# Another order and spacing of weight transforms in a two-layer kernel, three groups begun on GpSimd

## The chip, the cores and the metric

The kernel runs on 1 core of one Trainium2 chip. The metric is the device time in microseconds of one execution; the figure is the median over several. Engines are called PE (TensorE), DVE (VectorE), ACT (ScalarE), POOL (GpSimd) and SP (SyncE, which here only issues transfers).

## The reference, cut to what matters

2048 tokens of width 512 go through four blocks, each on the layer norm of the running x and added to x:

```
x = x + scan(ln(x))      # state space scan, 16 states per channel
x = x + ffn(ln(x))       # x' = fwht(x * SU)/64 ; silu(x' Wg^T) * (x' Wu^T) ; fwht ; Wd^T
x = x + mixer(ln(x))     # ((x Wx^T) conv^T * D) * silu(x Wz^T), then Wout^T
x = x + moe(ln(x))       # 64 experts, top 8, capacity 128
```

fwht is the Walsh-Hadamard transform over the last dimension. The kernel moves both transforms from the activations onto the weights: W_gate, W_up (u groups) and W_down (d groups) are transformed once, while the scan of the first tokens runs, and stored to HBM. In the same way W_in and conv_w of the mixer are multiplied into one matrix (the folds).

## The kernel before, in words

The tokens are done in 4 chunks of 512. The scan of a chunk takes 16 states, n = 0 to 15, and its work is spread over 4 places per state. A place is a number, pos = 5 + 64c + 4n + m for chunk c, state n and m = 0 to 3; (n,m) is used for a place of chunk 0. Each engine's program runs over the places in the same order, and at each one `side(pos)` issues the work of the other blocks that a table puts there. Engines are held together by semaphores alone.

In state n, DVE does **bx** (L1268, u times the broadcast of B in a PSUM bank), side(n,0), two scans (L1277), side(n,1), two scans, side(n,2), **hc** (L1295, bx times the broadcast of C), side(n,3). hc(n) below is its end. ACT makes the decay factors of the four blocks (L940); the one of block k waits for scan k-2, and blocks 2 and 3 stand between side(n,0) and side(n,1), blocks 0 and 1 of the next state ahead of side(n,3). PE makes the broadcasts of B (L662) and C (L670); the C broadcast of state n waits for hc(n-1). POOL adds hc to y (L1453). In chunk 0 PE and ACT also prepare chunk 1: transposes (ACT L902) in states 5 and 6, the product xdbl (PE L682) in state 7, softplus (ACT L912 to L923) in states 9 and 10.

Side work of chunk 0:

* **Preps.** A prep is one 128x512 tile of a transformed weight, 4 to a group, and there are 8 u groups and 4 d groups. PE does four fp32 matmuls with a plus or minus Hadamard matrix into a bank (L632), at the prep's place. One place later ACT writes the rounded hi part (L871, L874) and DVE the rest, the **lo** part (L1157, L1162). Two places later SP stores both (L382, L385), once the lo is done. The staging of d has two slots, so its hi waits for the store of the prep two before.
* **Butterflies.** A d group is first scaled and summed on POOL, in place: part 0 is one operation of 128x2048 (L1473), parts 1 and 2 are two of 128x1024 each (L1483). The next raw_d is loaded after the group's last prep. The table `butterflies` gives the place of each part.
* **Plains.** 16 tiles of W_in and W_out only split in hi (ACT L878, in fst) and lo (POOL L1489, one place later); SP stores them 3 places after, behind the prep's store of that place. fst has two slots: the hi of plain i waits for the store of plain i-2 (`mixer_hi`).
* **Folds.** 4 in chunk 0, places in `fold_at`: 8 matmuls each of winx and conv (L644), hi on ACT (L878), lo on DVE (L1169). SP loads conv (L410) and winx (L453) two places after the last prep's place, behind the wait for its lo, its store and the wait for its matmuls. At place 61 SP starts to load transformed weights back (ring).

Before: the preps have the places 3 to 50, one each, in the order u d u u u d u u d u u d; the plains have 7, 10, 13 to 52; the folds 58, 61, 64, 67.

Of the kernel before, what the change touches and what calls it, by code (L numbers as in the profile page):

```python
# [13 lines left out]
P = 128  # L14
# [3 lines left out]
KT = D // P  # L18
# [34 lines left out]
def build(nc, a):  # L53
# [5 lines left out]
    ALU, ACT, AX = mybir.AluOpType, mybir.ActivationFunctionType, mybir.AxisListType  # L59
    ds = bass.ds  # L60
    top = ExitStack()
    sem = lambda n: top.enter_context(nc.semaphore(n))

    def wait(eng, s, v):

        if not (isinstance(v, int) and v <= 0):
            eng.wait_ge(s, v)

    def sb(ctx, name, shape, dt=fp32):
        return ctx.enter_context(nc.sbuf_tensor(name, shape, dt))  # L70
# [30 lines left out]
    with top:  # L101
# [20 lines left out]
        with A:  # L122
# [32 lines left out]
            with ExitStack() as prep_only:  # L155
                staged_u = sb(prep_only, "staged_u", [P, 2, 4, 512], f32r)
                staged_d = sb(prep_only, "staged_d", [P, 2, 2, 512], f32r)
                raw_u = sb(prep_only, "raw_u", [P, 2, 4, 512])
                raw_d = sb(prep_only, "raw_d", [P, 2, M0 * P])
                wsdp = sb(prep_only, "wsdp", [P, D])  # L160
                had = sb(prep_only, "had", [P, 2, P])
            rawd, sums = raw_d[:, 0, :], raw_d[:, 1, :]
            ring = sb(A, "ring", [P, RING, 2 * D], f32r)
            expert_buffers((4,))
# [43 lines left out]
            PB, PC, dA, PF = bank[0], bank[1], bank[2:4], bank[4:8]  # L208
# [2 lines left out]
            S_x = [sem(f"x_in{c}") for c in range(NCH)]; S_id = sem("identity_in"); S_w = sem("weights_in")  # L211
            S_raw = [sem("raw_in0"), sem("raw_in1")]; S_rawd = sem("raw_down_in")
            S_wsc = sem("raw_scaled"); S_pmm = sem("prep_mm"); S_ph = sem("prep_hi"); S_pl = sem("prep_lo")
            S_bf = sem("butterfly"); S_sel = sem("selectors")
            S_su = [sem(f"up_stored{i}") for i in range(4)]; S_sd = [sem(f"down_stored{i}") for i in range(2)]
            S_wx = sem("winx_in"); S_cv = sem("conv_in"); S_pr = [sem(f"plain_in{i}") for i in range(4)]
            S_fm = sem("fold_mm"); S_mh = sem("mixer_hi"); S_fl = sem("fold_lo"); S_wl = sem("plain_lo")
# [24 lines left out]
            state_at = lambda c, n, m: HEAD + SPAN * c + 4 * n + m  # L242
# [27 lines left out]
            for place in range(TAIL, TAIL + RING):  # L270
                del quanta_at[place]

            kinds = [w for w in "uduuuduuduud"]
            group_of = [kinds[:i].count(kinds[i]) for i in range(len(kinds))]
            prep_places = list(range(3, 3 + 4 * len(kinds)))
            prep_at = {place: (i // 4, i % 4) for i, place in enumerate(prep_places)}
            fold_at = {state_at(0, 13, 1) + 3 * m: (0, m) for m in range(KT)} | {state_at(1, 1, 0) + 2 * m: (1, m) for m in range(KT)}
            FOLDS, PLAINS = 2 * KT, 2 * M1
            plain_at = {state_at(0, 0, 2) + 3 * i: i for i in range(PLAINS)}

            borrowed_b, borrowed_c = {}, {}
            for c in range(NCH):
# [56 lines left out]
            with nc.Block() as block:  # L339
# [17 lines left out]
                def _(sp):  # L357
# [17 lines left out]
                    def store_prep(i, m):  # L375

                        g = group_of[i]
                        sp.wait_ge(S_pl, 4 * i + m + 1)
                        if kinds[i] == "u":
                            for part in range(2):  # L380
                                dst = gate_up[g // 4, 4 * (g % 4):4 * (g % 4) + 4, :, m, part, :].rearrange("t p c -> p t c")
                                sp.dma_start(dst, staged_u[:, part, m, :].rearrange("p (t c) -> p t c", t=4).bitcast(fp32)).then_inc(S_su[m], 16)  # L382
                        else:
                            for part in range(2):
                                sp.dma_start(down_ffn[m, part, g],  # L385
                                             staged_d[:, m % 2, part, :].rearrange("p (x c) -> p x c", x=4).bitcast(fp32)).then_inc(S_sd[m % 2], 16)
# [55 lines left out]
                    def prep(pos):  # L442
                        if pos - 2 in prep_at:
                            i, m = prep_at[pos - 2]
                            store_prep(i, m)
                            g = group_of[i] + (2 if kinds[i] == "u" else 1)
                            if m == 3 and g < kinds.count(kinds[i]):
                                sp.wait_ge(S_pmm, 4 * i + 4)
                                load_raw(kinds[i], g)
                            if (i, m) == (len(kinds) - 1, 3):  # L450
                                sp.wait_ge(S_pmm, 4 * len(kinds))
                                load_conv(0)
                                sp.dma_start(winx[:, :, :], a["winx"].rearrange("(k p) h -> p k h", p=P)).then_inc(S_wx, 16)  # L453
                        if pos - 2 in fold_at:
                            half, m = fold_at[pos - 2]
                            sp.wait_ge(S_fl, KT * half + m + 1)
                            store_mixer(PLAINS + KT * half + m)
                            if half == 0 and m == KT - 1:
                                load_conv(1)
# [36 lines left out]
                    for pos in range(LAST):  # L496
# [11 lines left out]
                        if state_at(1, 8, 0) <= pos < state_at(3, 0, 0) and (pos - state_at(1, 8, 0)) % 6 == 0:  # L508
                            n = (pos - state_at(1, 8, 0)) // 6
# [46 lines left out]
                def _(pe):  # L556
# [65 lines left out]
                    def prep(i, m):  # L622
                        g = group_of[i]
                        if kinds[i] == "u":
                            pe.wait_ge(S_raw[g % 2], 16 * (g // 2 + 1))
                        else:
                            pe.wait_ge(S_bf, 4 * g + 4)
                        wait(pe, S_pl, 4 * (i - 1) + m + 1)
                        for k in range(4):
                            x = raw_u[:, g % 2, k, :] if kinds[i] == "u" else \  # L630
                                rawd.rearrange("p (x m h) -> p x m h", x=4, m=4)[:, :, k, :]
                            last = nc.tensor.matmul(PF[m][:, :], had[:, 0 if H4[m][k] > 0 else 1, :], x,  # L632
                                                    start=(k == 0), stop=(k == 3))
                        last.then_inc(S_pmm, 1)
# [811 lines left out]
                def _(pool):  # L1446
# [38 lines left out]
                    def plain_lo(i):  # L1485
                        pool.wait_ge(S_mh, i + 1)
                        s = i % 2
                        wait(pool, S_ms[s], 32 * (i // 2))
                        nc.gpsimd.tensor_tensor(fst[:, s, 1, :], praw[:, i % 4, :], fst[:, s, 0, :].bitcast(fp32),  # L1489
                                                ALU.subtract).then_inc(S_wl, 1)  # L1490

                    def correction(c, k):

                        pool.wait_ge(S_rs, KT * c + k + 1)
                        pool.wait_ge(S_rel, KT * c + k + 1)
                        nc.gpsimd.tensor_tensor(spc[:, k % 2, :], dl[c % 2][:, k, :], spc[:, k % 2, :], ALU.subtract).then_inc(S_co, 1)
                        pool.wait_ge(S_co, KT * c + k + 1)
                        nc.gpsimd.tensor_tensor(spr[:, k, :], spr[:, k, :], spc[:, k % 2, :], ALU.add).then_inc(S_sp, 1)
# [6 lines left out]
                    def states(c):  # L1505
                        for n in range(NS):
                            for m in range(4):
                                side(state_at(c, n, m))
                                if state_at(c, n, m) - 1 in plain_at:
                                    plain_lo(plain_at[state_at(c, n, m) - 1])  # L1510
                                if c >= 1 and (n, m) == (1, 2):
                                    norm_rstd(pool, n2, c - 1)
                                if c >= 1 and (n, m) == (14, 0):
                                    norm_rstd(pool, n3, c - 1)
                                if c + 1 < NCH:
                                    if (n, m) == (4, 1):
                                        norm_rstd(pool, n1, c + 1)
                                    if n in (9, 10) and m == 3:
                                        correction(c + 1, 2 * n - 18)
                                        correction(c + 1, 2 * n - 17)  # L1520
                                    if (n, m) == (13, 1):
                                        softplus_sum(c + 1)
                                if c == 0 and (n, m) in butterflies:
                                    butterfly(*butterflies[n, m])
                            add(c, n)

                    butterflies = {(2, 1): (1, 0), (3, 1): (1, 1), (4, 1): (1, 2), (6, 1): (2, 0), (6, 3): (2, 1), (7, 1): (2, 2),
                                   (9, 0): (3, 0), (9, 1): (3, 1), (10, 0): (3, 2)}

                    def rows_out(i, k):  # L1530
                        if (i, k) == (0, 0):
# [93 lines left out]
```

## Time and profile before

| | |
|---|---|
| median of 3 runs (lowest, highest) | 1737.85 us (1732.64, 1740.98) |
| the profiled execution, its own time | 1744.28 us |
| its span, first to last instruction | 1742.4 us |
| mean granted TensorE clock | 0.940 of full |
| busy: PE, DVE, POOL, ACT | 86%, 61%, 46%, 33% of the span |

The busy shares are means over stages that differ. Chunk 0, where the changed work lies, is the first sixth of the span; the last third belongs to the experts. A time in the trace counts from the span's start.

### The profile page before, as it was taken

How to read it: one execution, taken by the hardware profiler on the slowest of the kernel's cores; microseconds unless marked ns; L12 is line 12 of the kernel's file. 1: busy time of each engine (PE TensorE's matmuls, PEld its weight loads, DVE VectorE, ACT ScalarE, POOL GpSimd, SP SyncE). 2: the span in 40 equal slices, each digit the busy share in tenths (PEclk: the TensorE clock that was granted, in tenths of full speed). 3: DMA queues.
4: the chain of work that ended last, by engine and by line, in shares of the span. 5: the costliest groups of instructions: out<-in, count | busy, mean ns of one | idle time of the engine just before them, and what ended most of it. 6: DMA issues, size and time to landing. Idle time of an engine off the chain costs nothing. (4 is left out here: it accounts for less than half of the span.)

```text
span 1742.4 us, 19092 instructions
## 1 busy us (share of the span) xinstructions
PE 1506.9 (86%) x5792; PEld 1038.0 (60%) x5792; DVE 1062.9 (61%) x1591; ACT 583.2 (33%) x1034; POOL 794.6 (46%) x491
## 2 busy tenths in 40 slices
PE   6989966899948899988999899999991799998992
PEld 2444323577736677766887787778771455554551
DVE  4887688887898987889988746452553122222220
ACT  4434633344534335343433322121210232222220
POOL 3467853354744445634644326662376232222222
PEclk8999988999969999999999999999995899999996
DMA  6899663356644677766655468997760799999987
GB/s 202 251 280 277 194 217 132 101 156 196 199 140 149 201 221 222 216 192 225 187 183 169 145 201 305 351 317 227 227 191 25 227 329 317 311 306 301 307 211 126
DMA packets 193541, 380.41 MB, mean 218 GB/s; under 512 B 20994, under 2 KB 95106, under 8 KB 192944
## 3 DMA queue, kind: packets, MB, share of 16 engines
q1 hardware_dynamic: 165360, 322.89, 59.8%
q0 software_dynamic: 20032, 39.92, 9.7%
q10 hardware_dynamic: 8064, 16.55, 2.8%
q8 instruction: 42, 0.69, 0.2%
q14 instruction: 43, 0.35, 0.1%
HBM read 301.65 MB, written 124.35 MB: 244 GB/s over the span
## 5 line engine op out<-in xcount | busy, mean ns | idle before, releaser
L1453 POOL TENSOR_TENSOR y<-y,hc 128x2048 f32<-128x2048 f32 x64 | 293.3, 4582 | 250.3 <-DVE hc L1295 250.3
L590 PE MATMUL bank<-tokT,ring 128*128 128x512 f32 x768 | 307.9, 401 | 12.9 <-DVE xall L1150 6.9
L1277 DVE TENSOR_TENSOR_SCAN bx<-bank,state,bx 128x512 f32<-128x512 f32 x256 | 312.6, 1267 | 0.8
L592 PE MATMUL bank<-tokT,ring 128*128 128x512 f32 x768 | 302.3, 394 | 0.0
L591 PE MATMUL bank<-tokT,ring 128*128 128x512 f32 x768 | 302.2, 393 | 0.0
L940 ACT ACTIVATE bank<-dl,an 128x512 f32<-128x512 f32 x256 | 171.0, 684 | 330.4 <-DVE bx L1277 330.3
L1459 POOL TENSOR_TENSOR act<-th,act 128x512 fp32r<-128x512 f32 x96 | 126.4, 1316 | 269.6 <-ACT act L864 269.1
L819 PE MATMUL bank<-wgu,xeT 128*128 128x384 f32 x512 | 181.0, 498 | 0.0
L590 PEld LDWEIGHTS bank<-tokT,ring 128*128 128x128 f32 x768 | 146.2, 190 | 49.2 <-issue 17.6
L602 PE MATMUL bank<-ring,act 128*128 128x512 f32 x360 | 147.6, 410 | 22.6 <-DVE th L1139 17.3
L592 PEld LDWEIGHTS bank<-tokT,ring 128*128 128x128 f32 x768 | 146.0, 190 | 32.1
L591 PEld LDWEIGHTS bank<-tokT,ring 128*128 128x128 f32 x768 | 146.1, 190 | 29.4
L1295 DVE TENSOR_TENSOR hc<-bx,bank 128x2048 f32<-128x2048 f32 x64 | 146.0, 2282 | 22.7 <-PE bank L670 22.0
L1268 DVE TENSOR_TENSOR bx<-u,bank 128x2048 f32<-128x2048 f32 x64 | 146.0, 2281 | 9.5 <-PE bank L662 6.3
L1535 POOL DMA_INDIRECT slots<-row,idx x128 | 126.4, 987 | 38.4 <-issue 35.9
L604 PE MATMUL bank<-ring,act 128*128 128x512 f32 x360 | 143.4, 398 | 0.0
L603 PE MATMUL bank<-ring,act 128*128 128x512 f32 x360 | 143.3, 398 | 0.0
L1569 POOL DMA_INDIRECT out<-ye,tok x32 | 49.4, 1542 | 187.6 <-ACT ye L1087 110.5
L1132 DVE SCALAR_TENSOR_TENSOR th<-th,bank 128x512 f32<-128x512 f32 x96 | 65.7, 684 | 99.9 <-ACT th L859 88.9
L819 PEld LDWEIGHTS bank<-wgu,xeT 128*128 128x128 f32 x512 | 94.3, 194 | 53.5 <-issue 4.4
L836 PE MATMUL bank<-wde,hT 96*128 96x512 f32 x256 | 120.6, 593 | 0.5 <-DVE hT L1435 0.5
L632 PE MATMUL bank<-raw_u,had 128*128 128x512 f32 x256 | 115.5, 601 | 0.5 <-DMA raw_u<-wgT_in 0.5
(147 smaller groups left out, 2007.9 us busy)
## 6 DMA issues: line engine op xcount, KB each, us to landing
ring<-w_all SPq DMA_DIRECT2D x288, 512.0 KB
wgu<-wgu_in SPq DMA_DIRECT2D x64, 768.0 KB
wde<-wd_in SPq DMA_DIRECT2D x64, 384.0 KB
slots<-empty_in SPq DMA_DIRECT2D x16, 1154.0 KB, 8.7
w_all<-staged_u SPq DMA_DIRECT2D x64, 256.0 KB, 3.2
xe<-slots ACTq DMA_DIRECT2D x56, 288.5 KB
w_all<-fst SPq DMA_DIRECT2D x48, 256.0 KB, 3.7
w_all<-staged_d SPq DMA_DIRECT2D x32, 256.0 KB, 3.7
```

What stands on the lines that cost most here:

```text
L590: nc.tensor.matmul(b[:, :], w[:, k, 0, :], x[:, 0, k, :], start=(k == 0), stop=False)
L591: nc.tensor.matmul(b[:, :], w[:, k, 0, :], x[:, 1, k, :], start=False, stop=False)
L592: last = nc.tensor.matmul(b[:, :], w[:, k, 1, :], x[:, 0, k, :], start=False, stop=(k == KT - 1))
L602: nc.tensor.matmul(PF[t][:, :], act8[:, 0, j, tok], w[:, 0, :], start=(j == 0), stop=False)
L603: nc.tensor.matmul(PF[t][:, :], act8[:, 0, j, tok], w[:, 1, :], start=False, stop=False)
L604: last = nc.tensor.matmul(PF[t][:, :], act8[:, 1, j, tok], w[:, 0, :], start=False, stop=(j == pairs - 1))
L819: last = nc.tensor.matmul(CG[i % 2][:, 0:2 * FE], xeT[:, i % 2, k, :], wgu[i][:, k, :], start=(k == 0), stop=(k == KT - 1))
L940: nc.scalar.activation(dA[k % 2][:, :], dl[c % 2][:, k, :], ACT.Exp, scale=an[:, k, n:n + 1]).then_inc(S_dA, 1)
L1268: nc.vector.tensor_tensor(bx[:, :, :], u[:, :, :], PB[:, :].unsqueeze(1).to_broadcast([P, KT, CH]), ALU.mult).then_inc(S_bm, 1)
L1277: nc.vector.tensor_tensor_scan(bx[:, k, :], dA[k % 2][:, :], bx[:, k, :], state[:, k, n:n + 1], ALU.mult, ALU.add).then_inc(S_sc, 1)
L1295: nc.vector.tensor_tensor(hc[:, :, :], bx[:, :, :], PC[:, :].unsqueeze(1).to_broadcast([P, KT, CH]), ALU.mult).then_inc(S_cm, 1)
L1453: nc.gpsimd.tensor_tensor(y[c % 2][:, :, :], y[c % 2][:, :, :], hc[:, :, :], ALU.add).then_inc(S_ya, 1)
```

## The change

The order of the groups and the places of preps, plains, butterflies and folds are changed. The u groups with index 2, 5 and 8 are done in two stages: POOL forms the sums and differences of the raw halves (two operations of 128x1024 each, in a new tile `paired`), and a prep of these groups is then two matmuls of those. Its raw_u tile is loaded anew after the two sums and not after the matmuls. The Hadamard signs come out the same: rows 0 and 1 need the sums, rows 2 and 3 the differences.

```diff
+                paired = sb(prep_only, "paired", [P, 2, 2, 512])
-            kinds = [w for w in "uduuuduuduud"]
+            kinds = [w for w in "uduuduuduuud"]
-            prep_places = list(range(3, 3 + 4 * len(kinds)))
+            prep_places = [3 + 50 * i // 47 for i in range(4 * len(kinds))]
-            fold_at = {state_at(0, 13, 1) + 3 * m: (0, m) for m in range(KT)} | {state_at(1, 1, 0) + 2 * m: (1, m) for m in range(KT)}
+            PAIRED = [2, 5, 8]
+            paired_before = {i: PAIRED.index(i) for i in PAIRED}
+            pairs_at = {prep_places[4 * i] - 4 + 2 * part: (i, part) for i in PAIRED for part in range(2)}
+            fold_at = {state_at(0, 13, 2) + 5 * m // 2: (0, m) for m in range(KT)} | {state_at(1, 1, 0) + 2 * m: (1, m) for m in range(KT)}
-            plain_at = {state_at(0, 0, 2) + 3 * i: i for i in range(PLAINS)}
+            plain_at = {place: i for i, place in enumerate((7, 9, 11, 13, 20, 22, 24, 26, 32, 34, 36, 50, 52, 54, 56, 58))}
...
-                            if m == 3 and g < kinds.count(kinds[i]):
-                                sp.wait_ge(S_pmm, 4 * i + 4)
+                            if m == (0 if i in paired_before else 3) and g < kinds.count(kinds[i]):
+                                if i in paired_before:
+                                    sp.wait_ge(S_pd, 2 * paired_before[i] + 2)
+                                else:
+                                    sp.wait_ge(S_pmm, 4 * i + 4)
                                 load_raw(kinds[i], g)
...
+                        if i in paired_before:
+                            for k in range(2):
+                                last = nc.tensor.matmul(PF[m][:, :], had[:, k * (m % 2), :], paired[:, m // 2, k, :],
+                                                        start=(k == 0), stop=(k == 1))
+                            last.then_inc(S_pmm, 1)
+                            return
...
+                    def pair_sums(i, part):
+                        g = group_of[i]
+                        pool.wait_ge(S_raw[g % 2], 16 * (g // 2 + 1))
+                        if i != PAIRED[0]:
+                            pool.wait_ge(S_pmm, 4 * PAIRED[paired_before[i] - 1] + 2 * part + 2)
+                        nc.gpsimd.tensor_tensor(paired[:, part, :, :], raw_u[:, g % 2, 0:2, :], raw_u[:, g % 2, 2:4, :],
+                                                ALU.subtract if part else ALU.add).then_inc(S_pd, 1)
...
-                    butterflies = {(2, 1): (1, 0), (3, 1): (1, 1), (4, 1): (1, 2), (6, 1): (2, 0), (6, 3): (2, 1), (7, 1): (2, 2),
-                                   (9, 0): (3, 0), (9, 1): (3, 1), (10, 0): (3, 2)}
+                    butterflies = {(2, 1): (1, 0), (2, 3): (1, 1), (3, 1): (1, 2), (5, 2): (2, 0), (6, 0): (2, 1), (6, 2): (2, 2),
+                                   (9, 0): (3, 0), (9, 3): (3, 1), (10, 2): (3, 2)}
```

Written out, the preps of after have the places 3 to 18, 20 to 35, 37 to 51 and 53 (19, 36 and 52 are empty). The d groups stand at 7 to 10, 20 to 23, 32 to 35 and 49, 50, 51, 53; the paired u groups at 11 to 14, 24 to 27 and 37 to 40, and their pair sums at 7 and 9, 20 and 22, 33 and 35. The folds stand at 59, 61, 64 and 66.

## Rows read from the trace of the kernel before

**Rows 1.** Instructions in time on DVE, chunk 0: start, duration, operation, idle before.

```profile
44.95 2.29 DVE L1268 TENSOR_TENSOR bx<-u,bank 128x2048 f32<-128x2048 f32 x1
...
97.91 2.28 DVE L1295 TENSOR_TENSOR hc<-bx,bank 128x2048 f32<-128x2048 f32 x1
...
131.51 2.29 DVE L1295 TENSOR_TENSOR hc<-bx,bank 128x2048 f32<-128x2048 f32 x1
...
164.21 2.29 DVE L1295 TENSOR_TENSOR hc<-bx,bank 128x2048 f32<-128x2048 f32 x1 [1.14 <-PE bank L670]
...
208.65 0.75 DVE L1157 SCALAR_TENSOR_TENSOR staged_u<-bank,vec,staged_u 128x512 fp32r<-128x512 f32 x1 [5.29 <-ACT staged_u L871]
...
216.03 2.29 DVE L1295 TENSOR_TENSOR hc<-bx,bank 128x2048 f32<-128x2048 f32 x1 [3.33 <-PE bank L670]
...
282.83 2.28 DVE L1268 TENSOR_TENSOR bx<-u,bank 128x2048 f32<-128x2048 f32 x1
```

**Rows 2.** Stretch table: length, busy PE, PEld, DVE, ACT, POOL, clock, DMA share, GB/s.

```profile
44.90:226.20 181.30, 173.56 (x418) 77.89 (x416) 140.94 (x126) 87.40 (x152) 121.10 (x52) 0.98 0.85 247
```

**Rows 3.** Instructions in time on DVE, states 2 and 12.

```profile
74.25 2.28 DVE L1268 TENSOR_TENSOR bx<-u,bank 128x2048 f32<-128x2048 f32 x1
...
80.98 0.75 DVE L1157 SCALAR_TENSOR_TENSOR staged_u<-bank,vec,staged_u 128x512 fp32r<-128x512 f32 x1 [1.43 <-ACT staged_u L871]
...
87.51 2.28 DVE L1268 TENSOR_TENSOR bx<-u,bank 128x2048 f32<-128x2048 f32 x1
...
231.46 2.29 DVE L1268 TENSOR_TENSOR bx<-u,bank 128x2048 f32<-128x2048 f32 x1 [0.20 <-DVE hc L1295]
...
241.17 2.29 DVE L1268 TENSOR_TENSOR bx<-u,bank 128x2048 f32<-128x2048 f32 x1 [0.20 <-DVE hc L1295]
```

**Rows 4.** Instructions in time on PE, states 2 to 4.

```profile
80.53 0.79 PE L662 MATMUL bank<-xdr,sel 128*128 128x512 f32 x1
...
95.47 0.80 PE L662 MATMUL bank<-xdr,sel 128*128 128x512 f32 x1
...
111.00 5.40 PE L632 MATMUL bank<-raw_d,had 128*128 128x512 f32 x8 [4.21 <-POOL raw_d L1483]
```

**Rows 5.** Instructions in time, winx load (SP), fold 0 (PE) and its lo (DVE).

```profile
230.64 0.85 SPq L453 DMA_DIRECT2D winx<-winx_in  x1
...
245.31 8.52 PE L644 MATMUL bank<-conv,winx 128*128 128x512 f32 x16 [3.49 <-DMA winx<-winx_in]
...
254.50 0.69 DVE L1169 TENSOR_TENSOR fst<-bank,fst 128x512 fp32r<-128x512 f32 x1 [6.20 <-ACT fst L878]
```

**Rows 6.** The page's costliest groups: busy, mean ns of a record, idle before.

```profile
L632 PE MATMUL bank<-raw_u,had 128*128 128x512 f32 x256 | 115.5, 601 | 0.5 <-DMA raw_u<-wgT_in 0.5
```

**Rows 7.** Instructions in time, POOL and DVE in the head.

```profile
23.25 9.55 POOL L1483 TENSOR_TENSOR raw_d<-raw_d 128x1024 f32<-128x1024 f32 x4
...
30.63 2.72 DVE L1197 TENSOR_TENSOR spc<-dl,spc 128x512 f32<-128x512 f32 x1
...
34.45 0.69 DVE L1197 TENSOR_TENSOR spc<-dl,spc 128x512 f32<-128x512 f32 x1
```

**Rows 8.** Instructions in time, POOL and PE in states 6 and 7.

```profile
149.97 4.53 POOL L1453 TENSOR_TENSOR y<-y,hc 128x2048 f32<-128x2048 f32 x1
153.48 3.60 PE L682 MATMUL bank<-y,wxp 128*128 128x512 f32 x8
154.46 4.66 POOL L1483 TENSOR_TENSOR raw_d<-raw_d 128x1024 f32<-128x1024 f32 x2
```

**Rows 9.** DMA issues of the whole run: size, median us to landing.

```profile
winx<-winx_in SPq DMA_DIRECT2D x1, 2048.0 KB, 14.6
```

**Rows 10.** DMA queue and issues of 59 to 104 us.

```profile
q1 hardware_dynamic: 20813, 12.86, 101.4%
...
w_all<-fst SPq DMA_DIRECT2D x8, 256.0 KB, 4.8
```

**Rows 11.** Instructions in time on ACT, state 1.

```profile
67.21 0.60 ACT L874 ACTIVATE staged_d<-bank 128x512 fp32r<-128x512 f32 x1 [1.57 <-DMA w_all<-staged_d]
```

More of the change, by code:

```diff
@@ L213, in build @@
             S_wsc = sem("raw_scaled"); S_pmm = sem("prep_mm"); S_ph = sem("prep_hi"); S_pl = sem("prep_lo")
-            S_bf = sem("butterfly"); S_sel = sem("selectors")
+            S_bf = sem("butterfly"); S_pd = sem("pairs_summed"); S_sel = sem("selectors")
             S_su = [sem(f"up_stored{i}") for i in range(4)]; S_sd = [sem(f"down_stored{i}") for i in range(2)]
@@ L624, in prep @@
                         if kinds[i] == "u":
-                            pe.wait_ge(S_raw[g % 2], 16 * (g // 2 + 1))
+                            if i in paired_before:
+                                pe.wait_ge(S_pd, 2 * paired_before[i] + m // 2 + 1)
+                            else:
+                                pe.wait_ge(S_raw[g % 2], 16 * (g // 2 + 1))
                         else:
@@ L628, in prep @@
                         wait(pe, S_pl, 4 * (i - 1) + m + 1)
+                        if i in paired_before:
+                            for k in range(2):
[3 more added lines that the diff above has]
+                            return
                         for k in range(4):
@@ L1510, in states @@
                                     plain_lo(plain_at[state_at(c, n, m) - 1])
+                                if state_at(c, n, m) in pairs_at:
+                                    pair_sums(*pairs_at[state_at(c, n, m)])
                                 if c >= 1 and (n, m) == (1, 2):
```

## The prediction

> **What bounds the kernel now.** I read the busy table by stretches first, then VectorE (DVE) in order of time, then the engines it waits for. Every step the change touches lies in the head or in chunk 0, between the first bx at 44.95 us and chunk 1's first at 282.83 [rows 1]; up to place 53 TensorE (PE) looks like the bound: 173.6 us busy of 181.3, DVE 140.9 [rows 2]. The reader should distrust that share. In state 2, with four preps and no late input, DVE goes from bx to bx in 87.51 - 74.25 = 13.26 us, of which 1.43 is a wait for ScalarE (ACT) [rows 3]: the hi half of the prep at (n,0) stands on ACT behind the decay of block 3, and that behind DVE's second scan, while DVE does this prep's lo before its third scan. That wait is there however fast PE is. PE's own period with four preps is 95.47 - 80.53 = 14.94 [rows 4]. So PE exceeds the DVE-ACT loop by only 1.7 us a state, and may run up to some 6.6 us ahead (its next prep is needed only after a lo, bx, a lo, two scans and a decay: 0.7 + 2.2 + 0.7 + 2.4 + 0.7 by the same rows). A state without preps takes 241.17 - 231.46 = 9.7 [rows 3], so four lo cost 13.26 - 1.43 - 9.7 = 2.1, 0.53 each. Shorter preps alone therefore give back little; what counts is where DVE waits for PE, GpSimd (POOL) or a DMA, and where the chunk ends: PE waits for winx, the fold comes late, DVE stands 6.20 us [rows 5].
>
> **The change, part by part.** Times are of the profiled execution (span 1742.4, own time 1744.28, which is 6.4 above the median 1737.85); I carry the difference to the median.
>
> *Removed:* 3 groups x 4 preps x 2 matmuls = 24 fp32 matmuls. 128 such instructions make 256 records and 115.5 us busy, 0.90 each [rows 6]; between the broadcasts at 80.53 and 95.47 an unhindered prep of four takes some 3.43, 0.86 each, so 20.6 us of PE. Six POOL pair sums of 128x1024 come in, 2.37 each by the butterfly's row (9.55 for four of that size) [rows 7], 14.2 us. ACT and DVE do exactly as much as before.
>
> *Head.* The first pair sum (place 7) waits for nothing but the second raw_u load, one of the first transfers of all. POOL does it right behind the first butterfly, at 32.8 us. There DVE has its first softplus, and the rows show what meets: the subtraction that overlaps the last butterfly takes 2.72 us against 0.69 for the same one later, and ends 0.5 us after POOL [rows 7]. DVE is the chain there. A 2.37 us pair sum started in one of its gaps costs between 0 and 2.4; I take 2: **+2.0**. The trace shows two operands in SBUF on both sides. The Trainium skill, page SBUF — State Buffer, section "SBUF: two separate sides", states the rule: a DVE operation with two SBUF inputs and a GpSimd operation that reads SBUF hold the shared port pair exclusively, and the later one blocks for the whole instruction; by it this sum costs up to 2.4, and the other five nothing, since scans, bx, hc and lo read one operand from PSUM. The trace agrees (2.72 against 0.69); the sum above goes by the rows alone.
>
> *hc(3) to hc(5)* (100.19 to 133.80, each the start plus 2.28 or 2.29) [rows 1]: PE's 4.21 us wait for butterfly g1 [rows 4] goes, since the butterfly now runs before norm_rstd; place 19 is empty. DVE then needs, in state 4, 9.7 + 1.6 (three lo) + 3.9 for chunk 1's statistics + 1.3 ACT wait + 0.6 plain = 17.0 or so, and in state 5 9.7 + 2.1 + 3.1 (ACT wait with two evacuations and a plain ahead of the hi) = 14.9: 31.9 for 33.6: **-1.7**.
>
> *hc(5) to hc(7)* (133.80 to 166.50 = 32.7) [rows 1]: group 7 (d) begins at place 32 and needs butterfly g2, whose parts 1 and 2 both stand behind add(5). The chain is add 4.54, four butterfly halves 2 x 4.68 [rows 8], two preps 7.0, xdbl 3.4 [rows 8], two preps 6.5, broadcasts 0.9, hc 2.3: 34.1: **+1.4**.
>
> *hc(7) to hc(11)* (166.50 to 231.26, where hc(11) ends 0.2 before bx(12)) [rows 1, 3]: state 8 has one lo fewer, -0.3. In states 9 and 10 the long waits (5.29 in state 10) are ACT's softplus, six activations ahead of the hi, and stay; hc(10)'s wait of 3.33 for the C broadcast, on PE itself behind butterfly g3, goes [rows 1], with 0.6 for a plain no longer there and 1.4 of small PE waits: -5.3. State 11 gets a plain before its hi: +0.6. Together **-5.0**.
>
> *hc(11) to chunk 1.* Before, the winx load was issued at 230.64, 0.6 before hc(11), and PE started fold 0 at 245.31, when it had landed [rows 5]; 14.6 is its time to landing, conv ahead of it [rows 9]. Both loads stand in SP's program behind the store of the **last prep**, now place 53 = (12,0), whose lo DVE does at (12,1): after hc(11) a lo, bx, two scans, a decay, a plain and a hi (with its DMA wait), a lo: 8.4; store and two issues 1.5: winx at +9.9, landed +24.5. Fold 0 takes 8.0 to the next broadcast, folds 1 and 2 with their broadcasts 7.3 each, fold 3 7.0, hi and lo 1.4, delta_x 2.3, hc 2.3, bx: +60.9. Before: 282.83 - 231.26 = 51.6. **+9.3**. DVE arrives at its fold 0 lo at about +21.8 and stands some 12 us, where it stood 6.20 [rows 5]. The later fold places (59, 61, 64, 66) don't help: the data is late, not the place.
>
> Sum so far: 2.0 - 1.7 + 1.4 - 5.0 + 9.3 = **+6**.
>
> *Plains.* Before they were 3 places apart, now 2 in bunches. A plain's hi on ACT waits for the store of the plain two before, which SP issues 3 places after that plain, behind a prep's store. At spacing 2 that leaves one place. Queued behind ACT's wait are the prep's hi and the decays, and DVE waits for those. No such wait is in the trace (spacing 3 hides it): its lower bound is 0. In 59 to 104 us the queue is full (101.4%) and an fst store lands in 4.8 [rows 10]; a staged_d store issued behind a raw_u load held ACT until 67.21 [rows 11], some 7.6 after its issue. lo, two issues and landing make 5.7 to 9; ACT is there 3.9 to 5 after the lo. Plain 2: 1; plain 3, behind both the raw_d and the raw_u load that now fall in places 12 and 13: 4 to 6; plains 6 and 10: 2 each; upper end 12. Nearest to the rows taken in the full queue I take **+9**. Plains 13 to 15 fall under the winx wait and cost nothing; were it gone, plain 14's wait for a store queued behind 4.2 MB would show.
>
> After chunk 0 the program is the same and takes its start from it, so the sum passes on: **+15**, 1752.9.
>
> **Rivals.**
> *A. The plain waits are hidden* (DVE slack or quick stores), the head partly: +4 to +6, 1743. For it: ACT is idle a third of each state. Against: the full queue.
> *B. PE is the bound throughout* and ACT's wait is only its echo: the 20.6 us come off wholly before hc(11), the winx term stays: 20.6 - 9.3 = -11.3, 1726.6. It decides if states with paired preps fall to about 10 us. For it: the 173.6 of 181.3. Against: the 13.26 with PE on time.
> *C. The queue decides:* what is full now is asked for in bunches; every store that ACT waits for takes 7.6 or more, the plain term goes from 9 to 12 and the butterflies' d loads and the winx landing take some 2 more each: +22, 1760.
> *D. The change doesn't do what it says:* Hadamard rows 0,1 and 2,3 share sums and differences, so two matmuls suffice, and each is awaited by its own pair count; no chance worth a number.
>
> **Numbers.** About 0.5% (8.7 us) is what a measurement of this kernel can tell from no change. Forecast (+9 to +19) 0.50, A 0.25, B 0.12, C 0.13. Slower: forecast and C, 0.62 with the edge taken off; same: A and that edge, 0.26; faster: B, 0.12. The range goes from below A's end, -4, to C's near part, +27: 1734 to 1765.
>
> **What would show it.** In the profile after: bx(1,0) near 297 us instead of 282.8; winx issued near 9 to 10 us after hc(11) and fold 0's lo preceded by 10 to 14 us idle on DVE; no L632 wait for raw_d at states 4 and 10; one softplus operation of some 2.4 us more in the head; new ACT waits of fst on a DMA, the longest in state 2; states with paired preps still near 13 us. If those states take 10 to 11, the argument is wrong; if no ACT fst line names a DMA, the plain term is; if winx is issued before hc(11) + 5, the tail is.

## The result and the profile after

The changed kernel took 1764.63 us (median of 4, 1748.59 to 1768.74) where the kernel before took 1735.24; the ratio is 1.0147, 95% interval 1.0092 to 1.0202. It is slower. The medians lie 29 us apart, the ratio makes it some 25, and 15 were forecast; the median lies 0.4 us inside the upper end of the range (1765), so that the range held by luck. Timed again, the changed kernel took 1758.81 us, ratio 1.014 (below). Its profiled execution has a span of 1766.9 us for the 1742.4 before. Chunk 0 is 18.0 us of these 24.5.

DVE in order of time, after (start, duration, operation, idle before and its releaser), to be laid beside [rows 1, 3, 5]; L1284 is bx, L1293 the scan, L1311 hc, L1173 the u lo, L1185 the fold lo:

```profile
46.75 2.29 DVE L1284 TENSOR_TENSOR bx<-u,bank 128x2048 f32<-128x2048 f32 x1
...
84.36 0.75 DVE L1173 SCALAR_TENSOR_TENSOR staged_u<-bank,vec,staged_u 128x512 fp32r<-128x512 f32 x1 [6.94 <-ACT staged_u L887]
...
105.83 2.28 DVE L1311 TENSOR_TENSOR hc<-bx,bank 128x2048 f32<-128x2048 f32 x1
...
138.22 0.75 DVE L1173 SCALAR_TENSOR_TENSOR staged_u<-bank,vec,staged_u 128x512 fp32r<-128x512 f32 x1 [5.16 <-ACT staged_u L887]
...
141.90 2.28 DVE L1311 TENSOR_TENSOR hc<-bx,bank 128x2048 f32<-128x2048 f32 x1
...
177.60 2.29 DVE L1311 TENSOR_TENSOR hc<-bx,bank 128x2048 f32<-128x2048 f32 x1 [1.35 <-PE bank L686]
...
237.66 2.28 DVE L1311 TENSOR_TENSOR hc<-bx,bank 128x2048 f32<-128x2048 f32 x1
...
266.32 2.46 DVE L1293 TENSOR_TENSOR_SCAN bx<-bank,state,bx 128x512 f32<-128x512 f32 x2 [8.83 <-ACT bank L956]
...
274.03 0.69 DVE L1185 TENSOR_TENSOR fst<-bank,fst 128x512 fp32r<-128x512 f32 x1 [2.88 <-ACT fst L894]
...
300.84 2.29 DVE L1284 TENSOR_TENSOR bx<-u,bank 128x2048 f32<-128x2048 f32 x1 [0.20 <-DVE hc L1311]
```

From the ends of hc, the stretches of the forecast come out like this (us; the forecast's plain term is put where the plains are; "again" is the second profile of the changed kernel, from the experiment further down):

| stretch | before | after | change | forecast | again |
|---|---|---|---|---|---|
| start to first bx | 44.95 | 46.75 | +1.8 | +2.0 | 46.90 |
| to hc(3) | 55.2 | 61.4 | +6.1 | +5 to 7 (5 in the sum) | 61.7 |
| hc(3) to hc(5) | 33.6 | 36.1 | +2.5 | +0.3 | 36.1 |
| hc(5) to hc(7) | 32.7 | 35.7 | +3.0 | +1.4 | 34.0 |
| hc(7) to hc(11) | 64.8 | 60.1 | -4.7 | -3.0 | 60.1 |
| hc(11) to chunk 1's first bx | 51.6 | 60.9 | +9.3 | +9.3 | 60.3 |
| sum | | | +18.0 | +15 | |

The 24 matmuls are gone all the same: in chunk 0 PE is busy 10 us less than before, in 16 us more. Stretch table, kernel before and then after (length, busy PE, PEld, DVE, ACT, POOL, clock, DMA share, GB/s):

```profile
44.95:282.83 237.88, 207.23 (x490) 92.34 (x488) 188.04 (x158) 110.14 (x188) 146.35 (x59) 0.94 0.79 235
```

```profile
46.75:300.84 254.09, 197.07 (x437) 86.15 (x435) 188.79 (x158) 109.37 (x188) 156.71 (x64) 0.88 0.75 224
```

The granted clock of the stretch fell from 0.94 to 0.88 of full, so that part of the time saved is given back at 1.2 GHz; PE is idle for 57 us of the stretch, before for 31.

The head, DVE and POOL in time, beside [rows 7]:

```profile
30.42 2.72 DVE L1213 TENSOR_TENSOR spc<-dl,spc 128x512 f32<-128x512 f32 x1
33.17 2.72 DVE L1215 TENSOR_TENSOR spr<-spr,spc 128x512 f32<-128x512 f32 x1
```

```profile
32.55 2.80 POOL L1514 TENSOR_TENSOR paired<-raw_u 128x1024 f32<-128x1024 f32 x1
```

A second softplus operation now takes 2.72 us for 0.69, and it ends 0.5 us after the pair sum.

ACT in time. Before, no ACT instruction waited for an fst store; after, six plains do:

```profile
70.53 0.63 ACT L894 ACTIVATE fst<-praw 128x512 fp32r<-128x512 f32 x1 [2.32 <-DMA w_all<-fst]
...
83.12 0.63 ACT L894 ACTIVATE fst<-praw 128x512 fp32r<-128x512 f32 x1 [9.58 <-DMA w_all<-fst]
...
265.07 0.63 ACT L894 ACTIVATE fst<-praw 128x512 fp32r<-128x512 f32 x1 [12.09 <-DMA w_all<-fst]
```

The first two are plains 2 and 3, the last plain 14. The chunk's waits by pair of engines (in total, times, longest) add up to:

```profile
ACT fst L894 <- DMA w_all<-fst: 29.2, 6, 12.1
```

Two of the others are plain 6 (1.78 us, at 126.00) and plain 7, which the forecast did not have:

```profile
136.98 0.63 ACT L894 ACTIVATE fst<-praw 128x512 fp32r<-128x512 f32 x1 [2.13 <-DMA w_all<-fst]
```

The tail, SP and PE in time, beside [rows 5]:

```profile
249.36 0.83 SPq L460 DMA_DIRECT2D winx<-winx_in  x1
```

```profile
252.56 0.80 PE L686 MATMUL bank<-xdr,sel 128*128 128x512 f32 x1 [9.28 <-DVE hc L1311]
263.78 9.59 PE L660 MATMUL bank<-conv,winx 128*128 128x512 f32 x16 [10.42 <-DMA winx<-winx_in]
```

hc(11) ends at 239.94, so winx is issued 9.4 after it (forecast 9.9) and fold 0 starts 23.8 after it (forecast 24.5).

### The profile page after: what moved, and what is told of

Read it like the earlier page. It is cut to its first block and busy times, and to the rows that moved or that the text cites. A ratio compares the mean times of both kernels' runs of the same rounds, so it can differ in the third digit from the quotient of the medians.

```text
span 1766.9 us, 19006 instructions
## 1 busy us (share of the span) xinstructions
PE 1501.3 (85%) x5744; PEld 1035.7 (59%) x5744; DVE 1065.6 (60%) x1591; ACT 582.9 (33%) x1034; POOL 808.7 (46%) x497
## 5 line engine op out<-in xcount | busy, mean ns | idle before, releaser
L1293 DVE TENSOR_TENSOR_SCAN bx<-bank,state,bx 128x512 f32<-128x512 f32 x256 | 312.7, 1266 | 9.7 <-ACT bank L956 8.8
L1311 DVE TENSOR_TENSOR hc<-bx,bank 128x2048 f32<-128x2048 f32 x64 | 145.9, 2280 | 20.7 <-PE bank L686 20.0
L1284 DVE TENSOR_TENSOR bx<-u,bank 128x2048 f32<-128x2048 f32 x64 | 145.9, 2279 | 13.1 <-PE bank L678 10.2
L1438 DVE TENSOR_SCALAR wsc<-xe 128x1 f32 (+1 forms) x64 | 9.7, 152 | 162.2 <-DMA out<-ye,tok 94.7
```

Source lines behind the costliest of these rows:

```text
L1284: nc.vector.tensor_tensor(bx[:, :, :], u[:, :, :], PB[:, :].unsqueeze(1).to_broadcast([P, KT, CH]), ALU.mult).then_inc(S_bm, 1)
L1293: nc.vector.tensor_tensor_scan(bx[:, k, :], dA[k % 2][:, :], bx[:, k, :], state[:, k, n:n + 1], ALU.mult, ALU.add).then_inc(S_sc, 1)
```

## The experiments

Chunk 0 repeats far better than the whole: two profiles of the kernel before have chunk 1's first bx at 282.83 and 282.82, two of the changed one at 300.84 and 299.12. So this instant is read in each profile, and the whole time is weighed only where rounds were run. Gains on the changed kernel are given against its first profile, 300.84; against its second, 299.12, each is 1.7 us less. The difference lies mostly in the stretch from hc(5) to hc(7) (35.7 and 34.0).

**Plains back at their old places.**

```diff
-            plain_at = {place: i for i, place in enumerate((7, 9, 11, 13, 20, ...))}
+            plain_at = {state_at(0, 0, 2) + 3 * i: i for i in range(PLAINS)}
```

> The changed kernel with the plains back at their old places, 3 apart (7, 10 to 52), nothing else. Chunk 1's first bx stands at 300.8 us in the changed kernel and at 282.8 before. Theory (ACT waits for the fst store of the plain two before, and DVE for ACT): the 6.9 us idle of DVE in state 2 goes, 1.6 between states 4 and 5, and some 2 in state 5; the ACT wait of 12.1 us for plain 14 in states 12 and 13 goes too, but there the winx load takes over. First bx of chunk 1 near 291, the kernel 9 to 11 us faster than the changed one. Rival (the transfer queue is full because of the raw loads, whatever the plains do): at most 3 us faster, 298 or later.

Measured: first bx of chunk 1 at 293.75, 7.1 earlier; one run 1750.65. DVE in time, the lo in state 2 and the first fold lo:

```profile
77.96 0.75 DVE L1173 SCALAR_TENSOR_TENSOR staged_u<-bank,vec,staged_u 128x512 fp32r<-128x512 f32 x1
...
266.92 0.69 DVE L1185 TENSOR_TENSOR fst<-bank,fst 128x512 fp32r<-128x512 f32 x1 [11.24 <-ACT fst L894]
```

The 6.94 us in state 2 are gone, and no ACT plain waits for a transfer any more. The gain is below the expected 9 to 11. Up to hc(5) it is 8.5 us, where 10.5 were expected, and from hc(5) to hc(7) it takes 37.7 us for 35.7: PE comes earlier to the next d group, waits 4.37 us for its butterfly (3.13), and its 16 records take 9.56 us. What plain 14's wait had cost DVE (8.83 us) turns wholly into waiting for the fold (11.24 for 2.88): the two lay under one another, as forecast.

**Loads early.** conv and winx no longer stand behind the last prep. winx's memory overlaps the preparation buffers, so these were put in another order, with a gap of 2816 words before winx, and what is left to overlap is raw_u's second slot and `paired`, done with after group 10:

```diff
-                            if (i, m) == (len(kinds) - 1, 3):
-                                sp.wait_ge(S_pmm, 4 * len(kinds))
-                                load_conv(0)
-                                sp.dma_start(winx[:, :, :], ...)
+                        if pos == 43:
+                            load_conv(0)
+                        if pos == 51:
+                            sp.wait_ge(S_pmm, 44)
+                            sp.dma_start(winx[:, :, :], ...)
```

> The changed kernel with conv loaded at place 43 and winx at place 51 (behind the matmuls of group 10 alone), made possible by another order of the preparation buffers and a gap ahead of winx; nothing else is moved. Theory (the fold is late because its loads stand behind the last prep's store): PE no longer waits 10.4 us for winx, DVE's scans of state 13 no longer 8.8 us for ACT, since plain 12's store isn't queued behind 4 MB; from hc(11) to chunk 1's first bx 60.9 us become 48 to 52, first bx near 290. Rival (the folds' own PE time and places set it): 57 or more, first bx at 297 or later.

Measured: first bx at 294.27, 6.6 earlier; from hc(11) 54.3 us for the 60.9. The rival (57 or more) falls, but the gain is smaller than expected, and DVE shows why:

```profile
251.48 0.69 DVE L1180 TENSOR_TENSOR staged_d<-bank,staged_d 128x512 fp32r<-128x512 f32 x1 [5.54 <-ACT staged_d L892]
```

The winx load now runs in front of plain 11's store, ACT waits 3.61 for that, and the last prep's lo comes 5.5 late. The wait moved; part of it was paid twice.

**First pair sum one place later.**

```diff
+            pairs_at = {prep_places[4 * i] - 4 + 2 * part + (i == 2 and part == 0): (i, part) ...}
```

> The changed kernel with the first pair sum one place later (8), so that POOL does it behind plain 0's lo and not during DVE's first softplus. Theory (two operations with both operands in SBUF don't overlap): the second softplus operation takes 0.69 us and not 2.72, chunk 0's first bx is back from 46.75 to 44.95, all behind it 1.8 us earlier. Rival (the delay is from ACT or PE): no change at chunk 0's first bx.

Measured: chunk 0's first bx at 44.83 (1.9 earlier), and the second softplus operation 0.69. That part is shown. But chunk 1's first bx is at 295.36, 5.5 earlier and not 1.8: plain 3's wait fell from 9.58 to 7.98, and another 1.7 came off between hc(5) and hc(7). The latter is scatter: that stretch is 34.0 us here and in the changed kernel's second profile too. Why a shift of 1.9 us shortens plain 3's wait wasn't followed up.

**No pairs.**

```diff
-            PAIRED = [2, 5, 8]
+            PAIRED = []
```

> The changed kernel without pair sums: all preps are four matmuls again, order and places stay. Theory (PE isn't the bound in these states; the loop of DVE and ACT is): head 1.8 us earlier, the preps' states at most some 4 us longer in all, first bx of chunk 1 between 299 and 303. Rival (PE is the bound, and the pairs have saved 20.6 us that something else ate): first bx at 315 or later.

Measured, DVE in time:

```profile
44.75 2.29 DVE L1284 TENSOR_TENSOR bx<-u,bank 128x2048 f32<-128x2048 f32 x1
...
299.32 2.29 DVE L1284 TENSOR_TENSOR bx<-u,bank 128x2048 f32<-128x2048 f32 x1 [0.20 <-DVE hc L1311]
```

With 24 matmuls more the chunk takes 254.57 us for 254.09 (252.22 in the changed kernel's second profile). The pairs save 0.5 to 2.4 us behind the first bx, where 20.6 us of PE were taken out, and cost 2.0 in the head. State 8, whose four preps are all paired in the changed kernel, takes 12.7 us from bx to bx with pairs (180.41 to 193.14) and without (177.35 to 190.07). PE as the bound (315 or later) falls for this schedule.

**The new plain places alone, on the kernel before.**

```diff
-            plain_at = {state_at(0, 0, 2) + 3 * i: i for i in range(PLAINS)}
+            plain_at = {place: i for i, place in enumerate((7, 9, 11, 13, 20, ...))}
```

> The kernel before with the changed kernel's plain places (7, 9, 11, 13, 20 to 26, 32, 34, 36, 50 to 58) and nothing else of the change. Theory: the ACT waits for fst stores appear here too, so the cost belongs to the bunching and not to pairs or group order; chunk 1's first bx goes from 282.8 to between 288 and 294, with one ACT wait of 6 to 10 us near state 2. Rival (the raw_d and raw_u loads that the changed kernel puts into neighbouring places make the wait): less than 3 us, 286 or earlier.

Measured: first bx at 294.36, 11.5 later than before, at the upper end; one run 1758.14 beside 1737.16. ACT in time:

```profile
80.00 0.63 ACT L878 ACTIVATE fst<-praw 128x512 fp32r<-128x512 f32 x1 [8.28 <-DMA w_all<-fst]
```

The wait belongs to the bunching: here the u load is 3 places further off and the wait is nearly as long. 8.0 of the 11.5 come before hc(11), and 3.5 after it, where plain 14 waits 9.11 us for a store behind winx. The wait for fold 0 of before (6.20 us [rows 5]) lies under it: DVE now waits at most 1.3 us for a fold.

**The new prep and fold places alone, on the kernel before.**

```diff
-            prep_places = list(range(3, 3 + 4 * len(kinds)))
+            prep_places = [3 + 50 * i // 47 for i in range(4 * len(kinds))]
-            fold_at = {state_at(0, 13, 1) + 3 * m: (0, m) ...
+            fold_at = {state_at(0, 13, 2) + 5 * m // 2: (0, m) ...
```

> The kernel before with the changed kernel's prep places (3 to 53, three left empty) and fold places (59, 61, 64, 66), old group order, old plains, no pairs. Theory: the last prep, and so the winx load, is some 10 us later against hc(11), and from hc(11) to chunk 1's first bx it takes 60 to 62 us for the 51.6 of before; the states up to 11 lose 0 to 4 us by the empty places; first bx at 288 to 293. Rival (a later fold is better hidden): 284 or earlier.

Measured: first bx at 287.55, 4.7 later; just below the expected 288, well above the rival's 284. hc(11) ends at 227.22, 4.0 **earlier** than before, where 0 to 4 later were expected. Most of it is one wait: before, hc(10) stood 3.33 us for the C broadcast, on PE behind the wait for butterfly g3 [rows 1]; now the last d group starts at place 49 for 47, PE waits for that butterfly behind the broadcast, and hc(10) does not wait. From there it takes 60.3 us (expected 60 to 62). DVE in time:

```profile
260.74 0.69 DVE L1169 TENSOR_TENSOR fst<-bank,fst 128x512 fp32r<-128x512 f32 x1 [11.72 <-ACT fst L878]
```

So the new places are a gain up to hc(11) and a larger loss behind it, by the loads tied to the last prep. Prep and fold places were moved together here and not one by one.

**Loads early on the kernel before** (winx at place 50, else as above).

> The kernel before with conv loaded at place 43 and winx at place 50, fold places unchanged. Theory: PE's 3.5 us wait for winx goes, fold 0 starts right behind the C broadcast of state 13, and since PE is then at half clock its lo is still some 3 us late: chunk 1's first bx from 282.8 to about 279, 3 to 4 us earlier. Rival: the 4 MB among the d preps delay their stores, and ACT's hi with them, by as much: no change or later.

Measured: first bx at 280.01, 2.8 earlier; one run 1735.88. The direction holds, the size is a little under.

**Three things undone at once** (plains, loads, first pair sum, as above).

> The changed kernel with three things undone at once: plains 3 apart, first pair sum one place later, conv and winx loaded early; order of groups, pairs, prep, butterfly and fold places are the changed kernel's. Theory (these three are the whole loss): chunk 1's first bx at 281 to 286, level with the kernel before. Rival (order and butterflies or the pairs cost by themselves): 290 or later.

Measured: first bx at 282.10, 18.7 earlier than the changed kernel and level with the one before. One by one the three gave 7.1, 6.6 and 5.5, 19.2 together; against the second profile 14.1 together where this run gives 17.0. So an overlap is not seen, and a small one not excluded. What is left of the change (order of groups, pairs, prep, fold and butterfly places) is level in sum, but not stretch by stretch: from hc(5) to hc(7) it takes 38.1 us for 32.7 before, 5.4 more, with PE waiting 4.37 us for the butterfly and its 16 records behind that taking 10.02 us at a granted clock of 0.70; from hc(7) to hc(11) 60.6 for 64.8, 4.2 less.

**The changed kernel again.**

> The changed kernel once more, timed in five rounds. Theory (the loss is in chunk 0's schedule, which repeats from run to run): first bx of chunk 1 at 300.8 within 1 us of the first profile; the steps of 1.5 to 2 us that came on top in chunks 1 to 3 may fall in other states. Time 18 to 25 us above the kernel before, ratio 1.010 to 1.015. Rival (a good part of the first result was scatter): ratio under 1.008.

Measured: 1758.81 us for 1736.75, ratio 1.014, interval 1.0095 to 1.0185; first bx at 299.12, 1.7 from the first profile and not within 1. The rival, that scatter made a good part of the loss, falls.

**A better kernel before.** Loads early (43, 50), and:

```diff
-            fold_at = {state_at(0, 13, 1) + 3 * m: (0, m) ...
+            fold_at = {54 + 3 * m: (0, m) ...
-            butterflies = {(2, 1): (1, 0), (3, 1): (1, 1), (4, 1): (1, 2), ... (9, 0): (3, 0), (9, 1): (3, 1), (10, 0): (3, 2)}
+            butterflies = {(2, 1): (1, 0), (2, 3): (1, 1), (3, 1): (1, 2), ... (9, 0): (3, 0), (9, 1): (3, 1), (9, 2): (3, 2)}
```

> The kernel before with conv and winx loaded early (places 43 and 50), folds at 54, 57, 60, 63, butterfly g1 parts 1 and 2 at (2,3) and (3,1), and g3's last part at (9,2), ahead of the corrections; no pairs, old plains. Theory: DVE's waits for the fold and PE's for butterflies g1 and g3 go; first bx of chunk 1 from 282.8 to between 270 and 276, the kernel 7 to 13 us faster than before. Rival (the folds then delay the C and B broadcasts, or the early loads the d stores): 279 or later, as with the early loads alone.

Measured: 1730.45 us for 1736.75, ratio 0.996, interval 0.9929 to 0.999; first bx at 276.55, 6.3 earlier, just short of what was expected. hc(11) gains 4.4 and the tail 1.9. It beats both kernels, by little.

**The same with the spread prep places** (winx at 51, folds at 56, 59, 62, 65).

> As e10, but with the changed kernel's prep places (3 to 53), winx at place 51 and folds at 56, 59, 62, 65. Theory: the empty places let DVE catch up before state 11 (6.1 us there by the new places alone) and the early load takes away what they cost at the end; first bx at 269 to 276, within 3 us of e10. Rival: the last prep's store behind winx holds ACT in state 12, 279 or later.

Measured: 1735.03 us, ratio 1.0004 (0.9972 to 1.0037); first bx at 278.94, within 3 us of the last experiment but short of the range. At hc(10) it is 1.2 us ahead of the kernel before, where the experiment with the places alone was 6.1 ahead. POOL in time:

```profile
189.73 4.55 POOL L1475 TENSOR_TENSOR raw_d<-raw_d,wsdp 128x2048 f32<-128x2048 f32 x1 [6.42 <-DMA raw_d<-wdT_in]
```

The third d group ends two places later, its next raw_d load with it, and butterfly g3 kept its place: POOL stands 6.42 us for the load, and what it does for the softplus of state 10 comes late behind the butterfly, whose last part is now ahead of it. DVE stands 2.37 us for ACT and 1.69 for POOL in that state. So here the spreading isn't worth its last prep at 53; with butterfly g3 moved along it wasn't tried.

**The kernel before again.**

> The kernel before, unchanged, for a second profile. From chunk 1's first bx to bx(12) of chunk 3 the first profile took 654.2 us, and the two of the changed kernel 660.0 and 661.5, though the program there is the same. Theory (the extra comes with where PE's granted clock falls and rises, which shifts with chunk 0's end but repeats with the same kernel): 653 to 656 again. Rival (it is scatter from run to run): another value between 654 and 663. Chunk 1's first bx at 282.8 within 1 us in both cases.

Measured: first bx at 282.82; from there to bx(12) of chunk 3 655.0 us, for 654.2 in the first profile. See below.

## Why the prediction was right, and where it was off

*The bound.* Right. That a state with four preps takes some 13 us whether PE has two or four matmuls a prep is what the run without pairs shows: 12.7 us either way in state 8, 0.5 to 2.4 us for 24 matmuls in all. That it is the loop of DVE and ACT which sets these 13 us is read from the rows and was not tried. The run shows the bound in the changed schedule alone, where other waits also hide PE; on a schedule without those the pairs weren't tried by themselves.

*Head.* +1.8 for +2.0. Moving the sum one place restored the first bx (44.83). The rule of the Trainium skill (SBUF — State Buffer, "SBUF: two separate sides"), that of a DVE operation with two SBUF inputs and a GpSimd operation that reads SBUF the later one blocks, held for this sum: 2.72 us for 0.69. That the other five sums cost nothing held in the changed kernel, but see the next point.

*hc(3) to hc(5).* +2.5, not +0.3, and here a step failed. The forecast had store waits for plains 6 and 10 but none for plain 7. It waited 2.13 us, the hi of a prep stood behind it on ACT, and DVE was idle 5.16 us in state 5 where I had put 3.1. With the plains at their old places this idle time is 2.40.

A second step failed and cost little: "PE's 4.21 us wait for butterfly g1 goes". Its absence was one of the signs asked for, and the wait is there. PE in time, after, and then with the plains at their old places:

```profile
104.13 9.20 PE L648 MATMUL bank<-raw_d,had 128*128 128x512 f32 x16 [4.90 <-POOL raw_d L1499]
```

```profile
100.66 9.09 PE L648 MATMUL bank<-raw_d,had 128*128 128x512 f32 x16 [8.00 <-POOL raw_d L1499]
```

The plain waits are not its cause, since without them it is longer (7.31 with three things undone). In the new order the second d group starts at place 20 instead of 23, so PE asks for butterfly g1 sooner, and its last part still stands on POOL behind the addition of hc(2). Nor does DVE wait for it between hc(3) and bx(4). What does cost DVE there, with the plains at their old places, is the last operation of chunk 1's statistics:

```profile
104.61 4.03 DVE L1136 TENSOR_SCALAR n_ngt<-n_mvt 128x4 f32<-128x4 f32 x1
```

It took 1.07 us before, 1.73 after and 3.22 with three things undone, and each time it ends with POOL's addition of hc(3). POOL comes to that addition late, behind the last part of the butterfly, plain los and the third pair sum. So what the spaced plains give in state 5 is in part lost in state 4.

*hc(5) to hc(7).* The chain named is the right one: PE waits for the butterfly. Its size was right where the profile repeats: 34.1 us were forecast, and 34.0 were measured in the second profile, without pairs, and with the first pair sum later. In the first profile it took 35.7 us; PE waited 3.13 us for the butterfly (1.76 in the second) and then ran its d preps partly at half clock, 16 records in 8.83 us (7.13 in the second), the first 12 of them here:

```profile
158.21 7.11 PE L648 MATMUL bank<-raw_d,had 128*128 128x512 f32 x12 [3.13 <-POOL raw_d L1499]
```

That the same stretch takes 37.7 and 38.1 us once the plain waits are gone was not in the forecast.

*hc(7) to hc(11).* -4.7 for -3.0: plain 10's wait (1.3 us) cost nearly nothing where 2 were put.

*Tail.* +9.3 for +9.3, and the mechanism is shown twice: the places alone give 60.3 us from hc(11), the early loads 54.3. The exact hit has luck in it. Fold 0 started 0.7 us sooner after hc(11) than forecast and took 9.0 us to the next broadcast for 8.0, the terms as they stand in the forecast add up to some 60.2 and not 60.9, and the second profile has 60.3.

*Plains.* The sixteen places alone cost 11.5 on the kernel before and give back 5.4 to 7.1 on the changed one; the term was 9, its upper end 12.

*Rivals.* A (the plain waits are hidden) falls with the plains at their old places, though ACT has more room than was put for it: it is busy 87.4 us of 181.3 [rows 2], so idle half of a state and not a third. B (PE is the bound) falls with the run without pairs. The forecast proper, +9 to +19, was missed: some +25 is nearer to C (the queue decides, +22). But what C gave as its reasons isn't there. winx landed in 14.4 us (14.6 before), and from 59 to 104 us an fst store landed in 4.5 us and the raw_d load in 6.9 in the median (4.8 and 7.1 before). 18.0 us of the 24.5 lie in chunk 0, inside the forecast, and most of the rest in what follows.

*Passing on.* "After chunk 0 the program is the same and takes its start from it, so the sum passes on" is the step that made the forecast 10 us too small rather than 3. From chunk 1's first bx to bx(12) of chunk 3 the kernel before takes 654.2 and 655.0 us in its two profiles, the changed one 660.0 and 661.5; it comes mostly in steps of 1.5 to 1.9 us within single states. State 12 of chunk 1, kernel before and then after:

```profile
467.06:477.64 10.58, 10.35 (x45) 8.56 (x46) 9.38 (x8) 6.98 (x8) 6.03 (x3) 1.00 0.52 146
```

```profile
483.08:495.45 12.37, 12.14 (x45) 9.94 (x46) 9.38 (x7) 7.90 (x9) 7.75 (x3) 0.83 0.44 126
```

The same 45 PE records take 1.8 us longer at a granted clock of 0.83 for 1.00. In both, PE is idle for 2.6 us until 3.4 us ahead of this state. In the kernel before its records drop to 1.2 GHz right behind that idle time (0.63 us for 0.39) and are back at 2.4 GHz 0.5 us into the state; in the changed one they drop only 0.8 us behind it and stay there until 4.2 us into the state:

```profile
483.88 0.63 PE L610 MATMUL bank<-ring,act 128*128 128x512 f32 x1
...
487.49 0.39 PE L610 MATMUL bank<-ring,act 128*128 128x512 f32 x1
```

In this state the step is therefore where the granted clock falls against the work. For the rest of the 6 us that is likely and was not read out, and the cause was not tried. The time at which chunk 0 ends does not settle it: the versions lie between 656 and 663 in no order with their shift (656.0 with the better kernel, 656.8 without pairs), and with three things undone chunk 0 ends 0.7 us from where it ended before and these chunks take 661.4. Nor is each state fixed by the kernel: state 12 of chunk 2 takes 10.58 and 12.17 us in the two profiles of the kernel before. So the size can't be told ahead. The rest, from bx(12) of chunk 3 to the end, is 806.1 and 795.8 us in the two profiles of the changed kernel, 805.4 and 797.6 in those of the one before: the same, with scatter.

## What to carry to other kernels

Before a spacing in a hand-written order is tightened, find the buffer that its old value hid: here two slots of fst, a store that is issued three places later, and an in-order engine on which everything else waits behind. Ask of each place that moves which transfers are issued behind it: the last prep's place was worth less than the 4 MB in line behind it. Where a group is moved forward, ask whether what prepares it moves too: here PE came to two d groups before their butterflies were done. And a busy share of 96% on one engine doesn't make it the bound where a loop of two others takes nearly as long.

## What the runs showed of the hardware that was not expected

A pair sum of 2.36 us beside DVE's softplus blocks one of its operations nearly whole (2.72 for 0.69), and its own record is longer too (2.80 for 2.36). A DVE operation of only 128x4, 0.17 us where POOL is idle (at 322.96 us, after), took 1.07 to 4.03 us beside POOL's addition of 128x2048 and ended with it each time. Stores of 2 x 256 KB issued behind a 1 MB load were awaited 9.6 us by ACT; two stores issued behind the 4 MB of conv and winx, 12.1. And the same program of chunks 1 to 3 took 6 us longer in both profiles of the changed kernel than in both of the one before, with the granted clock at its lower level in other places; what decides that stays open.
